# Four plain indirect requests of GpSimd under way, or one: a transformer block with routed feed-forward parts on one core

## The reference, cut to what matters

```python
def _fff(x, nw, nb, w1, b1, w2, b2, act):      # 8 levels, 256 leaves of width 16
    node = zeros
    for _ in range(8):
        logit = einsum('bsd,bsd->bs', x, nw[node]) + nb[node]
        node = 2 * node + 1 + (logit > 0)
    leaf = node - 255
    h = act(einsum('bsd,bsdl->bsl', x, w1[leaf]) + b1[leaf])
    return einsum('bsl,bsld->bsd', h, w2[leaf]) + b2[leaf]
q, k, v = _fff(xn, q_...), _fff(xn, k_...), _fff(xn, v_...)
att = softmax(einsum('bqd,bkd->bqk', q, k) / sqrt(256))
y = xn + einsum('bqk,bkd->bqd', att, v)
return y + _fff(y, f_..., gelu)
```

## Time and profile before

| | us |
|---|---|
| median of 3 runs | 1382.71 (1381.66 to 1383.93) |
| span of the profiled execution | 1503.4 |
| first request of q (POOL) | 510.1 |
| q, k and v end (last add of gq_) | 815.6 |
| attention, first turn of PE | 819.8 |
| first request of f | 920.6 |
| f ends (last add of gf_) | 997.1 |

### The profile page before, as it was taken

One profiled execution on the slowest core, in us unless ns is written; L12 is line 12 of the kernel. 1 busy time (PEld: TensorE's weight loads), 2 busy tenths in 40 slices (PEclk: granted clock), 3 DMA queues, 4 the chain that ended last, 5 costly groups with the idle time before them and its releaser, 6 DMA issues. The chain is left out here.

```text
span 1503.4 us, 24492 instructions
## 1 busy us (share of the span) xinstructions
PE 1203.0 (80%) x7028; PEld 869.8 (58%) x7032; DVE 887.9 (59%) x2553; ACT 580.3 (39%) x1116; POOL 466.2 (31%) x749
## 2 busy tenths in 40 slices
PE   2597999999857756584958793868999989999997
PEld 1395677777646545373746672655666645555554
DVE  8998999999234643452625363565766634453534
ACT  2324566665322113252635331634666641212110
POOL 2237344555450336326141704622221000000000
PEclk9858999999979978697978896876999999999999
DMA  9000000000007412383823731625100000000000
GB/s 267 0 2 1 1 1 1 1 1 1 1 8 192 143 43 80 107 252 97 262 80 91 259 101 56 96 70 136 16 13 10 2 1 1 14 0 14 0 14 15
DMA packets 92463, 91.98 MB, mean 61 GB/s; under 512 B 27057, under 2 KB 77747, under 8 KB 92341
## 3 DMA queue, kind: packets, MB, share of 16 engines
q1 hardware_dynamic: 80052, 65.32, 14.5%
q0 software_dynamic: 12288, 25.18, 6.8%
HBM read 75.79 MB, written 14.68 MB: 60 GB/s over the span
## 5 line engine op out<-in xcount | busy, mean ns | idle before, releaser
L2263 PE MATMUL gq_psH<-gq_xT,gq_w 128*128 (+1 forms) x564 | 102.9, 309 | 53.3 <-ACT gq_act L1981 28.4
L2263 PEld LDWEIGHTS gq_psH<-gq_xT,gq_w 128*128 128x128 f32 x564 | 83.4, 209 | 81.6 <-issue 76.6
L3503 ACT ACTIVATE m_silu<-m_psG 128x512 f32<-128x512 f32 x48 | 28.7, 597 | 215.3 <-PE m_psU L3623 215.3
L2273 PE MATMUL gq_psY<-leaf_w,gq_hT 128*128 (+1 forms) x282 | 95.2, 422 | 20.0 <-issue 14.3
L3556 DVE TENSOR_TENSOR m_act<-m_silu,m_psU 128x512 f32<-128x512 f32 x48 | 33.0, 687 | 122.5 <-ACT m_silu L3503 107.7
L1865 POOL DMA_INDIRECT gq_x<-rows_x,gq_token_i x48 | 47.0, 979 | 174.0 <-PE gq_psX L2252 105.6
L3623 PE MATMUL m_psG<-m_xnT,m_gate 128*128 128x512 f32 x192 | 91.2, 597 | 2.1 <-PEq L192 2.1
L3623 PE MATMUL m_psU<-m_xnT,m_up 128*128 128x512 f32 x192 | 91.4, 599 | 0.0
L2149 DVE SCALAR_TENSOR_TENSOR gq_hT<-gq_xT,unit_leaf,gq_act 128x128 f32<-128x128 f32 x141 | 49.6, 352 | 61.7 <-issue 28.6
L1981 ACT ACTIVATE gq_act<-gq_psH,leaf_b 128x128 f32<-128x128 f32 x141 | 51.4, 365 | 75.4 <-remote 41.5
L783 DVE MATCH_REPLACE8 s_product_a_rest<-a_top,s_product_a_rest 128x256 f32<-128x256 f32 x192 | 76.1, 408 | 0.3 <-issue 0.3
(11 more groups left out here) (574 smaller groups left out, 3063.6 us busy)
## 6 DMA issues: line engine op xcount, KB each, us to landing
leaf_w<-in_group_w SPq DMA_DIRECT2D x128, 128.0 KB
leaf_w<-in_group_w SPq DMA_DIRECT2D x64, 256.0 KB
a_w<-in_L_xattn_W SPq DMA_DIRECT2D x2, 1024.0 KB, 11.9
rows_x<-token_rows SPq DMA_DIRECT2D x8, 256.0 KB, 5.4
sorted_y_q<-gq_y SPq DMA_DIRECT2D x16, 128.0 KB, 3.9
sorted_y_k<-rows_ahead SPq DMA_DIRECT2D x16, 128.0 KB, 4.4
sorted_y_v<-gq_y SPq DMA_DIRECT2D x16, 128.0 KB, 1.7
rows_f<-token_rows SPq DMA_DIRECT2D x8, 256.0 KB
```

The source lines that it names most:

```text
L2263: last = pe.matmul(psH[n % 2][:, 0:P], w1[n % 3][:, c, :], xT[:, c, bass.ds(g * -P + u * P, P)], start=(c == 0), stop=(c == DC - 1))
L2273: pe.matmul(psY[n % 3][:, 0:D], hT[n % 2][:], weights.w2[:, bass.ds(g * D, D)], start=True, stop=True).then_inc(y_ps, 1)
```

## The change

The limit goes from four requests to one. Each of the 96 requests of q, k and v, the 16 gathers of f and the 32 requests of the attention then waits for the landing of the one just before it. Nothing else differs: the order, the rests, the buffers and all other waits stay, and `ahead.pool`, the biases of line 1693 and the later requests of line 2837 have no such limit in either kernel.

```diff
--- before.py
+++ after.py
@@ -1703,7 +1703,7 @@
         self.weights.load(sp)
 
 
-UNDER_WAY = 4
+UNDER_WAY = 1
 
 
 class Rests:
```

## The result

The changed kernel takes **1636.12 us** (median of 4 runs, 1630.34 to 1638.01) against 1383.32 before: ratio 1.182, 95% interval 1.179 to 1.185. That is 253 us slower. The recorded execution has a span of 1628.6 us and a time of 1630.34.

The account below looks back on a forecast made before the run. Units bound q, k and v, with requests covered by four under way. Waits add 31 + 35 + 4 + 6 = 76 us, and 118 us of profile-only delays come back: 1382.7 + 76 + 118 = 1577 us, range 1450 to 1640.

Parts of the forecast that it names:

- The late signals: Seven stretches of the recorded execution: PE's signals up to 8 us late under dense request bursts, 118 us, absent from timed runs.
- the first rival: Whole kernel: PE's signals late in timed executions too, so the change gives back 118 us: 1459 us, chance 0.14.
- What one request costs alone: POOL's gathers: a lone request takes c = 2.9 us in place of 1.29, and 4.5 us beside weight loads.
- The rivals on c: Cost of a lone request: 2.2 us gives 1360 us (chance 0.05); 4.1 us gives 1719 us (chance 0.05).
- q, k and v: 96 requests back to back, 14 at 4.5 and 82 at 2.9, 301 us; end at 847 in place of 815.6, +31.
- Attention and f: Attention: k's last turn +35 us from 30 requests, 103 us, plus +4 for cold starts; f: sixteen gathers, +6.
- What I had called covered: In f, bias requests until 998 and SP's moved loads and stores end with the units, adding no time.
- tile 11: In q, k and v: unit 8 waits some 32 us for this tile, whose gather stands behind sixteen seeds on POOL.
- the forecast of 1580: Span of the changed kernel's recorded execution: 76 us above the profiled 1503.4, about 1580.
- faster with a cheap request: Late signals in the time and a lone request of 2.2 us: 99 us less, 1360 us, chance 0.05.
- The dear request: A lone request takes 4.1 us even with idle DMA engines: 1719 us, chance 0.05.
- That the limit would do nothing: POOL's requests would not wait for each other, the landing being counted before the wait: 1383 us, chance 0.02.

Follow-up runs that it names:

- e1_same: The kernel before, unchanged, recorded again: time 1389.24 us, span 1387.5.
- e4_swapped: Changed kernel, limit one, with the ring-buffer or stored-tile wait moved behind the landing wait: 1611.68 us, ratio 1.165.
- e7_small_loads: Changed kernel, limit one, with only 16 columns of each weight load of k, v and f fetched: 1597.9 us.
- e3_paced: Kernel before, limit four, with two rests after each request in place of one: 1387.4 us, ratio 1.003.

## Why the prediction was right, and where it was short

**The late signals stand in no time.** Right in its result, and not shown in its cause. I took 118 us out of the recorded execution; stage by stage against e1_same it is 96.7 + 12.8 + 13.2 = 123 us, less 6.6 by which its front was shorter, 116. Without this step the forecast would have been 1459, the first rival, and 177 us short. But "under a long dense burst of requests" was a story made from one trace: e1_same has the same bursts and no late signal, so the step came out right partly by luck. The evidence that did hold was only arithmetic, that the stretches and the gap between span and median were nearly the same number.

**What one request costs alone.** 2.9 us forecast, 2.98 measured, with a landing of 2.7 to 2.8. The step held, on a single row at the start of f. By the Trainium skill ("DMA: Bandwidth & Descriptors", Anatomy of one DMA, SWDGE path) it would have been, as an estimate, between 2.3 and 3.25 us; the spacing lies between, and the landing is above 2.3. The rivals on c, at 2.2 and at 4.1, fell with it.

**q, k and v: the term that was too small.** 337 us forecast, 381 measured. The 95 spacings show where 44 us went: 35 of mean 2.98 (+3 against 2.9), 38 of mean 3.48 (+22), and 22 of mean 4.81, 106 us, where I had 14 at 4.5 and would have put 2.9 on the other 8, 86 us (+20). The 3.48 is the cost of two waits in a row, which no row of the kernel before shows: there a request with both waits starts 1.29 us after the last one, like the others. 18 of the 22 long spacings have both waits too, so the split into +22 and +20 is a rough one; e4_swapped checks it, with 22 us less in the sum of the spacings (24 in the time) and 22 above my forecast left. Those are the loads: I counted seven requests to a load of 30 us, but SP issues k's weights over 48 us and v's over 37 (618.68 to 666.5 and 736.92 to 773.8), about as long as in e1_same (48 and 36), so the 30 was too short for either kernel. The stores of finished tiles lie there too (q's from 642.3 to 666.6). In e7_small_loads most of that went.

**Attention and f.** 30 requests were to take 103 us; PE's last turn of k starts at 1004.53, 107.0 us after the first request. The stage is 145.9 us for a forecast of 144, f 84.0 for 83. What I had called covered was covered: the biases of line 1693 and SP's loads and stores end with f's units.

**How the 59 us add up, and the range.** The recorded span is 48.6 us above the forecast of 1580: 44 in q, k and v, 2 in the attention, 1 in f and 1 before the first request. A further 5.8 are that this recorded execution lies below the median, 1.7 that a time is longer than its span, and 3 that I had 1580 for the span and 1577 for the time. The range held by its width: its upper end allowed 0.45 us more for each request, from whatever cause, and the requests of q, k and v used that up (3.60 us in the mean where I had 3.14). The pair of waits was not foreseen at all.

**What follows whom.** PE waits 36 us for tile 11 where 32 were forecast, and the end of q, k and v, 892.7, follows the landing of the last gather (853.51 + 2.8) by 36 us, as forecast. The dense burst of `ahead.pool` lies in these last units, as before the change, and shows no late signal.

**The rival with late signals in the time** (1459, or faster with a cheap request) fell with e1_same and e3_paced, whose recorded executions have no late signal and took 1389 and 1385 us, as the timed ones do. The dear request fell with the landing of 2.8 us. That the limit would do nothing fell with the first row.

## What to carry to other kernels

Before a limit on transfers under way is lowered, write down the period of the consumer, the time from issue to landing, and how many transfers a period needs: here 53 us, 3 us and 32, so that one under way needs 96 us, and two, with what stood beside them, 66. Look also at how many waits stand in a row before each request. Take the landing both with idle DMA engines and beside the loads that run at the same time. And record an execution twice when its span and the timed median disagree; a difference of 9% was here one disturbed record.

## What the runs showed of the hardware that I had not expected

Two waits in a row ahead of an indirect request of GpSimd cost 0.5 us after the last of them is met (3.48 against 2.98 us), if the one that is met last stands last. With the two exchanged, or with an IOTA between them that carries the first, the cost is gone. With both long met they cost 0.37 us in e3_paced (1.90 against 1.53) and nothing in e1_same (1.29).

A request of 128 rows of 1 KB lands 2.7 to 2.8 us after its issue in the median (2.6 at the least) when it is alone, and up to 5.7 us beside loads, where the DMA engines are busy for 0.82 (640 to 660 us) to 0.93 (740 to 760 us) of the time. With a single wait before it the next one starts 2.98 us after the last, some 0.2 to 0.3 us after the landing.

In one recorded execution ScalarE and VectorE started up to some 8 us after the matmuls that they needed, in seven stretches, and the three stages were 123 us longer than in e1_same. It did not come back in any of the 11 other recorded executions, with requests 1.29 us apart or 3.0. Its cause stays open. The gap between profile and reported time that the Trainium skill ("Runtime: NRT & Kernel Launch", The ~15µs preamble/postamble breakdown) puts at 6.2 us was -1.7 us in e1_same, span less time, and 120.7 us in that one record, against the median. The span runs from the first to the last instruction and is not the total time of which the page speaks, so neither number tests its figure, and the prediction compared unlike things there.
